# Gated cross-attention and ternary FFN on one core: attention turns of eight heads over two PSUM banks, and a norm over four batches with Newton steps on GpSimd

## The reference

```python
x = x + tanh(g_xattn) * attention(layernorm(x), ctx)   # q from x; k, v from ctx; softmax over the context; @ Wo
x = x + tanh(g_ffn) * (gelu(layernorm(x) @ ternary(W1).T + b1) @ ternary(W2).T + b2)
# layernorm(x) = (x - mean) / sqrt(var + 1e-5), over the 256 columns, no weights
```

## Time and profile before

| | us |
|---|---|
| median of 3 runs (lowest, highest) | 1670.24 (1670.09, 1671.91) |
| the profiled execution, its own time | 1668.12 |
| span of its instructions | 1666.3 |
| PE busy in the span | 1511.3 (91%) |
| DVE busy | 1487.7 (89%) |
| ACT busy | 938.2 (56%) |
| POOL busy | 668.6 (40%) |

### The profile page before, as it was taken

The page is one execution under the profiler, slowest core; times in us unless marked ns, Lnnn a source line. Parts: engine busy times, 40 slices in busy tenths (PEclk is TensorE's granted clock), DMA queues, the critical chain, the costliest instruction groups (busy, mean ns, idle before and its releaser), DMA issues.

```text
span 1666.3 us, 48258 instructions
## 1 busy us (share of the span) xinstructions
PE 1511.3 (91%) x14501; PEld 1010.6 (61%) x14501; DVE 1487.7 (89%) x4375; ACT 938.2 (56%) x1799; POOL 668.6 (40%) x813
## 2 busy tenths in 40 slices
PE   3899999999999999999999999997999999999998
PEld 2566666666666666666666666664666666666665
DVE  7799999999999999999999999987888888888886
ACT  2465656565656666566656565644555554555554
POOL 5355555455554545554555555452111111111111
PEclk9799999999999999999999999986999999999999
DMA  2333333333333333333333333311010110101101
GB/s 79 89 97 85 94 85 86 97 86 97 83 96 83 97 84 93 87 89 92 86 97 83 98 81 97 80 47 55 27 38 25 38 36 27 38 25 38 38 25 51
DMA packets 207471, 117.93 MB, mean 71 GB/s; under 512 B 24912, under 2 KB 207184, under 8 KB 207440
## 3 DMA queue, kind: packets, MB, share of 16 engines
q1 hardware_dynamic: 207440, 117.54, 26.1%
HBM read 32.53 MB, written 16.78 MB: 30 GB/s over the span
## 4 chain that ended last, share of the span: by engine, by line
PE 54%; DVE 26%; issue 13%; ACT 4%; DVEq 2%; DMA 0%; ACTq 0%
PE bank L1060 12%; PE bank L308 9%; PE bank L1090 5%; PE bank L1089 5%; DVE smax L745 5%; PE bank L332 4%; PE bank L315 4%; PE bank L299 4%; DVE xres L790 3%; DVE rstd L685 3%; DVE k L715 2%; DVE rstd L687 2%; PE bank L387 2%; DVE y L1047 2%; DVE rstd L678 2%
## 5 line engine op out<-in xcount | busy, mean ns | idle before, releaser
L915 POOL TENSOR_TENSOR probl<-prob 128x512 f16<-128x512 f32 x512 | 528.9, 1041 | 535.8 <-ACT prob L597 534.9
L597 ACT ACTIVATE prob<-bank,masks 128x512 f32<-128x512 f32 x512 | 345.2, 687 | 144.9 <-PE bank L367 144.9
L745 DVE TENSOR_REDUCE smax<-bank 128x4 f32<-128x512 f32 x512 | 348.1, 681 | 14.5 <-PE bank L332 10.6
L1076 DVE TENSOR_TENSOR hidl<-hid 128x512 f16<-128x512 f32 x256 | 226.9, 886 | 79.5 <-ACT hid L1071 78.8
L1071 ACT ACTIVATE hid<-bank,b_sb 128x512 f32<-128x512 f32 x256 | 175.9, 687 | 212.3 <-PE bank L1060 206.1
L1060 PE MATMUL bank<-y,w1T 128*128 128x512 f16 x1024 | 262.9, 379 | 29.9 <-DVE y L1047 28.4
L1154 POOL TENSOR_TENSOR xres<-xres,b2g 128x1024 f32 (+1 forms) x32 | 75.7, 2365 | 431.3 <-ACT yln L1024 413.4
L1089 PE MATMUL bank<-w2T,hid 128*128 128x256 f16 x1024 | 237.4, 273 | 1.4 <-ACT w2T L1004 1.4
L1090 PE MATMUL bank<-w2T,hidl 128*128 128x256 f16 x1024 | 237.3, 273 | 0.0
L332 PE MATMUL bank<-k_rows,q_rows 34*128 34x128 f16 x2048 | 228.0, 222 | 6.8 <-DMA q_rows<-smaxT 3.4
L367 PE MATMUL bank<-q_rows,k_rows 50*128 50x128 f16 x2048 | 204.4, 221 | 0.9 <-DMA q_rows<-smaxT 0.9
(11 more groups left out here) (90 smaller groups left out, 2555.7 us busy)
## 6 DMA issues: line engine op xcount, KB each, us to landing
q_rows<-q SPq DMA_DIRECT2D x512, 64.0 KB, 2.6
k_rows<-k SPq DMA_DIRECT2D x512, 64.0 KB, 2.5
xres<-in_x_dram SPq DMA_DIRECT2D x64, 256.0 KB, 2.7
out_dram<-ystage SPq DMA_DIRECT2D x32, 512.0 KB, 2.9
ctx_sb<-in_ctx_dram SPq DMA_DIRECT2D x64, 192.0 KB, 3.1
q_rows<-smaxT SPq DMA_DIRECT2D x128, 8.0 KB
w_raw<-in_L_ffn_W_dram SPq DMA_DIRECT2D x2, 1024.0 KB, 6.7
prob<-in_L_xattn_Wq_dram SPq DMA_DIRECT2D x1, 256.0 KB, 3.9
```

Source lines behind the costliest of these rows:

```text
L597: act.activation(prob[u][:], st_bank[u % 2][:], ACT.Exp, bias=0.0, scale=masks[g.parity][:, 2 + b:3 + b]).then_inc(exp_done, 1)
L745: dve.tensor_reduce(smax[:, b, u * UH:(u + 1) * UH], sm_bank[u % 2][:].rearrange("p (h j) -> p h j", h=UH), AX.X, ALU.max).then_inc(max_ta ...
L915: pool.tensor_tensor(probl[u][:], prob[u][:], prob[u][:].bitcast(BF16)[:, 1::2], ALU.subtract).then_inc(prob_split, 1)
```

## The change

- A batch has two turns of eight heads instead of four of four (`PH = 8`, `PAIRS = 2`). A turn's scores fill both banks of a pair (`sm_banks`, `st_banks`), and one `take_max` and one exponential read 1024 columns. Each pair is a single buffer: rough scores wait for the last maximum, scores for the last exponential. `low_prob` still runs on four heads at a time, and `weigh` waits for each half.
- `pe_group` and `dve_group` are written anew in this order. On VectorE, `add_attention` moves from its place behind one `take_max` to behind `take_max`, `round_max`, `low_max`, `read_weighed` and `normalise`, at both of its places in a group.
- The norm of x runs over four batches, once per two groups, in the group of parity 0. VectorE makes statistics and seed (`seed_x`, four parts: `norm(0)` to `norm(3)`), GpSimd the Newton steps (`root_x`, 14 parts, two behind each `low_prob` from the second on). `x` is loaded four batches at a time, and that load waits for `ln_ready`.
- In the FFN the same 14 parts remain on VectorE. The negative half of the variance is made one part earlier, and the wait for `y_done` moves from part 3 to part 12.

```diff
 def pe_group(pe, g, left):
-    scores(pe, g, 0, 0, (g, 1, 2))
+    scores(pe, g, 0, 0, (g, 1, 1))
     if not first:
-        weigh(pe, before, 1, 2)
+        weigh(pe, before, 1, 1)
         tr = project_out(pe, g.batch(0) - 2, tr)
-    scores(pe, g, 0, 1, (g, 1, 3))
-    if not first:
-        weigh(pe, before, 1, 3)
     if left >= 2:
         pe.wait_ge(v_split, g.n + 1)
         project_q(pe, g2, 0)
         tr = transpose_ctx(pe, g2, tr)
         project_q(pe, g2, 1)
-    scores(pe, g, 0, 2, (g1, 0, 0) if left >= 1 else None)
+    scores(pe, g, 0, 1, (g1, 0, 0) if left >= 1 else None)
+    tr = transpose_max(pe, g, 1, tr)
     weigh(pe, g, 0, 0)
-    tr = transpose_max(pe, g, 1, tr)
-    scores(pe, g, 0, 3, (g1, 0, 1) if left >= 1 else None)
-    weigh(pe, g, 0, 1)
...
-    scores(pe, g, 1, 0, (g1, 0, 2) if left >= 1 else None)
-    weigh(pe, g, 0, 2)
+    scores(pe, g, 1, 0, (g1, 0, 1) if left >= 1 else None)
+    weigh(pe, g, 0, 1)
     if not first:
         tr = project_out(pe, g.batch(0) - 1, tr)
-    scores(pe, g, 1, 1, (g1, 0, 3) if left >= 1 else None)
-    weigh(pe, g, 0, 3)
     if left >= 3:
         tr = transpose_x(pe, g.after(3), tr)
...
 def dve_group(dve, g, left):
-    take_max(dve, g, 1, 2)
-    norm(8)
-    if not first:
-        add_attention(dve, g.batch(0) - 2)
-    norm(9)
-    take_max(dve, g, 1, 3)
+    take_max(dve, g, 1, 1)
+    norm(0)
     round_max(dve, g, 1)
-    norm(10)
+    norm(1)
     low_max(dve, g, 1)
+    norm(2)
     if not first:
         read_weighed(dve, g.batch(0) - 1, 1, 1)
+        norm(3)
         normalise(dve, g.batch(0) - 1, 1, 1)
+        add_attention(dve, g.batch(0) - 2)
...
     if left >= 2:
         low_k(dve, g2)
-    if not first:
-        add_attention(dve, g.batch(0) - 1)
     if left >= 1:
-        take_max(dve, g1, 0, 3)
+        take_max(dve, g1, 0, 1)
         round_max(dve, g1, 0)
         low_max(dve, g1, 0)
     read_weighed(dve, g.batch(0), 0, 1)
     normalise(dve, g.batch(0), 0, 1)
+    if not first:
+        add_attention(dve, g.batch(0) - 1)
...
+def seed_x(dve, half, i):
+    past = half - 2
+    if i == 0:
+        dve.wait_ge(x_in, 16 * (half + 1))
+        for b in range(QB):
+            last = dve.bn_stats(stats[:, b, :], row_of(half * QB + b))
+    elif i == 1:
...
+        dve.tensor_copy(rstd[:, 2, :], stats[:, :, 1])
+        for b in range(QB):
+            last = dve.bn_aggr(meanvar[:, b, :], stats[:, b, :])
+    elif i == 2:
...
+        dve.tensor_scalar(newton[:, 2, :], meanvar[:, :, 1], EPS, -0.5, ALU.add, ALU.mult)
+        last = dve.tensor_scalar(newton[:, 0, :], meanvar[:, :, 1], EPS, None, ALU.add)
+    else:
...
+        dve.tensor_scalar(newton[:, 1, :].bitcast(I32), newton[:, 0, :].bitcast(I32), -0.5, RSQRT_SEED,
+                          ALU.mult, ALU.add).then_inc(root_seeded, 1)
+def root_x(pool, half, i):
...
+        elif i % 4 == 1:
+            last = pool.tensor_tensor(t, y, y, ALU.mult)
+        elif i % 4 == 2:
+            last = pool.tensor_tensor(t, t, hv, ALU.mult)
...
 def pool_group(pool, g, left):
     for b in range(2):
         for u in range(UNITS):
             low_prob(pool, g, b, u)
+            k = b * UNITS + u
+            if g.parity == 0 and left >= 4 and k >= 1:
+                for i in range(2 * k - 2, 2 * k):
+                    root_x(pool, g.half + 2, i)
 def sp_group(sp, g, left):
-    if left >= 4:
-        sp.wait_ge(ln_done, x_past)
-        load_x(sp, g.after(4))
+    if g.parity == 1 and left >= 6:
+        sp.wait_ge(ln_ready, x_past)
+        load_x(sp, g.half + 3)
```

More of the change, by code:

```diff
@@ L658, in ln_part @@
         def ln_part(dve, i, rows, step, base, ready):
-            n = len(rows)
-            half, y, t, shift = (rstd[:, k, 0:n] for k in range(4))
+            half, y, t = (rstd[:, k, :] for k in range(3))
             if i > 0:
@@ L693, in row_of, with norm_x @@
             return xres[:, bass.ds(batch, 1), :].rearrange("p o d -> p (o d)")
-        def norm_x(dve, g, parts):
+        def norm_x(dve, half, parts):
             for i in parts:
                 if i == 0:
-                    dve.wait_ge(x_in[g.parity], 16 * (g.half + 1))
-                if i == 3 and not (isinstance(g.half, int) and g.n == 0):
-                    dve.wait_ge(ln_done, 2 * g.n)
-                rows = [row_of(g.batch(b)) for b in range(2)] if i == 0 else (None,) * 2
-                ln_part(dve, i, rows, ln_step, g.n * (LN_PARTS - 1), ln_ready)
+                    dve.wait_ge(x_in, 16 * (half + 1))
+                if i == LN_PARTS - 2 and not (isinstance(half, int) and half == 0):
+                    dve.wait_ge(ln_done, QB * half)
+                rows = [row_of(half * QB + b) for b in range(QB)] if i == 0 else ()
+                ln_part(dve, i, rows, ln_step, half * (LN_PARTS - 1), ln_ready)
@@ L816, in dve_first @@
             dve.wait_ge(mask_set, 1)
-            norm_x(dve, g1, range(LN_PARTS))
             low_q(dve, g0)
@@ L860, in dve_group @@
             if not first:
                 read_weighed(dve, g.batch(0) - 1, 1, 1)
+                norm(3)
                 normalise(dve, g.batch(0) - 1, 1, 1)
-            norm(11)
+                add_attention(dve, g.batch(0) - 2)
+            else:
+                norm(3)
+            norm(4)
             if left >= 2:
                 low_q(dve, g2)
+            norm(5)
+            if left >= 1:
+                take_max(dve, g1, 0, 0)
+            norm(6)
+            read_weighed(dve, g.batch(0), 0, 0)
@@ new lines, in dve_group @@
+            norm(7)
+            normalise(dve, g.batch(0), 0, 0)
+            if left >= 2:
+                low_k(dve, g2)
+            norm(8)
+            if left >= 1:
+                take_max(dve, g1, 0, 1)
+                round_max(dve, g1, 0)
+            norm(9)
+            if left >= 1:
+                low_max(dve, g1, 0)
+            norm(10)
+            read_weighed(dve, g.batch(0), 0, 1)
+            norm(11)
+            normalise(dve, g.batch(0), 0, 1)
+            if not first:
+                add_attention(dve, g.batch(0) - 1)
@@ L1011, in norm_y @@
             for i in parts:
-                if i == 3 and not (isinstance(g.half, int) and g.n == 0):
-                    dve.wait_ge(y_done, QB * g.n)
-                rows = [row_of(g.n * QB + b) for b in range(QB)] if i == 0 else (None,) * QB
+                if i == LN_PARTS - 2:
+                    if isinstance(g.half, int) and g.n == 0:
+                        dve.wait_ge(ln_done, B)
+                    else:
+                        dve.wait_ge(y_done, QB * g.n)
+                rows = [row_of(g.n * QB + b) for b in range(QB)] if i == 0 else ()
                 ln_part(dve, i, rows, y_step, g.n * (LN_PARTS - 1), y_ready)
```

291 lines of the change are left out of this document (147 added, 144 removed).

## The result

The changed kernel takes 2047.35 us (median, 2044.29 to 2051.60) where the kernel before, run beside it, took 1670.16: a ratio of 1.2261 [1.2233, 1.2290], 377 us slower. The forecast was 2120 us, 73 too many. The profiled execution has a span of 2043.8 us at a mean granted clock of 0.822. The whole loss lies in the attention: from the first to the last start of ScalarE's gelu (tile `hid`) the FFN takes 503 us (1533.5 to 2036.1), and before it took 504 (1154.6 to 1658.6).

The account below looks back on a forecast made before the run. The prediction took chains from TensorE through ScalarE and VectorE, closing at the two transposes behind `add_attention`, as the bound. 1668 us plus 234 for later chains plus 222 for low clock gave 2124, say 2120 us; range 1850 to 2300.

Parts of the forecast that it names:

- The place of the loss: TensorE waiting for the late `add_attention` at the context and x transposes, 3 to 6 us a group together.
- First chain: Context transpose begins 4.75 us after ScalarE's `high_v` starts (A), 0.69 later than before; in parity 0 the seed adds 2.5.
- Second chain: x transpose begins 4.39 us after ScalarE's `high_k` starts (B), 2.29 us later than before, in every group.
- The sum at full clock: Attention groups grow 3.9 us on average over 60 groups: 234 us more, 1902 us without any fall of the clock.
- the 0.3 us that were to come back at the changes of turn: TensorE saves 0.3 us a group, between 0 and 0.7, through fewer changes of turn.
- The clock: TensorE's clock falls around the x transpose in most groups, costing 3.7 us a group, 222 us in all.
- five such pieces, two of them hidden: From x transpose to first quarter's end, five slow projection pieces cost 4.7 us; the first wait hides two, leaving 2.8.
- The rival with falls in parity 0 alone: The clock falls only in attention groups of parity 0, giving 2013 us; chance 0.08.
- What was costed at nothing: Exponentials and `low_prob`, `root_x` steps, SP's load of x behind `ln_ready`, single buffers; FFN and start within 5 us.
- The signs named: Profile: transposes wait 3 to 6 us a group, VectorE about 1240 us, below 70% in attention, mean clock near 0.8.
- The rival of three seed operations held up by `low_prob`: Up to three VectorE seed operations each wait for GpSimd's `low_prob`, 3.1 us in 30 groups: 94 us more, 2214 us.

Follow-up runs that it names:

- b1: The kernel before with only both `add_attention` moved behind `normalise`; four-head turns, double buffers and old norm stay: 2220.24 us, ratio 1.3309.
- e4: The changed kernel with useless float32 projections in TensorE's two pauses, the waits for `add_attention` kept: 1901.32 us, ratio 1.1402.
- e5: The changed kernel with both `add_attention` early and the load of x at the end of SyncE's group: 1803.00 us, ratio 1.0824.
- n1: The kernel before with only the new norm (four batches, Newton steps on GpSimd), load of x last in SyncE's group: 1659.15 us, ratio 0.9927.
- e8: e5 with useless float32 products ahead of each x transpose and at two places behind the seed in even groups: 1717.35 us, ratio 1.0294.
- e1: The changed kernel with both `add_attention` back at the head of their chains, the rest kept: 1864.65 us, ratio 1.1186.
- m1: The kernel before with only the eight-head turns, both `add_attention` early and the old norm: 1695.39 us, ratio 1.0164.
- n2: n1 with two useless float32 products at each of two places behind the seed in even groups: 1634.99 us, ratio 0.9792.

## Why the prediction was right, and where it was off

**The place of the loss** was right. b1 shows that the late `add_attention` alone makes a loss of this kind, and the transposes wait 3.8 us a group (3 to 6 were named).

**First chain.** Forecast A + 4.75 in parity 1; it was A + 5.23. The difference is one instruction: `low_max` took 0.92 instead of 0.17 us, and without these 0.75 it would be A + 4.48. In parity 0 it was A + 6.30 against 4.75 + 2.5 = 7.25: the seed cost 6.30 - 4.48 = 1.82, just under its lower bound of 1.9. Its copy took 0.17, where the row of before gave 0.57. That the two errors nearly cancel is luck: over both parities the place moved by (1.17 + 2.24) / 2 = 1.70 us, where 0.69 + 1.25 = 1.94 was forecast.

**Second chain.** Forecast B + 4.39, measured B + 4.30. The maximum of 1024 columns was put at 1.30 and takes 1.217.

**The sum at full clock.** Forecast +234 us; e4 measures +231. This closeness is in part luck. The groups of e4 take 20.2 and 21.3 us in turn, on average 3.9 more than the 16.84 before, as much as the 1.70 and 2.2 by which the two places moved. So the 0.3 us that were to come back at the changes of turn do not show; the two places, some 0.3 us together less late than forecast, make up for them.

**The clock.** This is the term that was mis-sized: 60 x 3.7 = 222 us forecast, 146 measured (2.4 a group). The step "five such pieces, two of them hidden" counted the second `project_q` as slow. In the rows above it runs at 1.03 us, since the clock was back by 727.9, and so it does in 14 of 15 groups between 500 and 860 us. That is 60 x 0.94 = 56 of the 76 us by which the term was too large. The rest is not parted: some stretches were back after only 3.4 us, others lasted 13.7 and more. The mechanism (fall around the x transpose, return in the float32 work of the next group's first half) is in the windows. In 200 to 400 us a mean of 0.78 means 44% of the time at 0.50.

The rival with falls in parity 0 alone does not stand. Groups of parity 1 fall as well: their x transposes at 738.28 and 786.22, behind pauses of 2.49 us, run in 1.11 us instead of 0.65. The Trainium skill (TensorE: Matmul & The Clock Gate, "HAM oscillation — how this bites in real kernels") ties the oscillation to long waits between bursts. The trace agrees as far as the clock oscillates, but here pauses of 0.3 to 0.8 us in a cluster (e5, n1) preceded falls too.

**What was costed at nothing.** In the changed kernel itself it cost nothing that shows. SyncE waits there for `ln_ready` too (55.5 us in 17 times from 200 to 1000 us), but no wait of TensorE for moved rows stands in that stretch, so the late chains cover it. Once they are mended, SyncE's queue behind `ln_ready` is worth 62 us (e5), and of the 133 us left in e5 86 or more are the low clock (e8). That an early `add_attention` would not bring the old time back was not seen: e1 gives back 183 of 377 us.

**The signs named.** Waits, VectorE's share (57%, below 70% was named) and mean clock (0.822, near 0.8) came out. VectorE's busy time fell to 1307.8 us, not 1240: 2.9 us fewer a group (16.0 to 13.1) where some 4 were forecast. The small parts that left had overlapped their neighbours in the busy time: from 400 to 800 us the groups of VectorE's instructions add up to 18.7 us a group before and 14.5 after, 4.2 fewer. The parities differ by 1.07 us at the first place, not 2 to 3, since the seed was shorter and `low_max` longer.

The rival of three seed operations held up by `low_prob` did not come about, and this trace is no test of it: in the pair shown no `low_prob` ran beside the seed's copy at 703.74 (the last two began at 701.42 and took 2.04 us), and all eight copies between 500 and 860 us took 0.17.

**What stays open.** Why m1's pauses nearly always leave the clock at 1.00 (two falls from 200 to 1000 us) and e5's, as large in the window shown, do not. In e5 the seed's pauses come in the group beside them, and filling both places (e8) holds the clock, but no run separates how the two add up.

## What to carry to other kernels

When a change frees an engine that looks full, look first at what stands ahead of the one instruction for which the bounding engine waits: here 2.9 us fewer a group on VectorE lost to some 2 us more ahead of each `add_attention`. Price the late instruction and the clock apart, by filling the pauses with useless matmuls: the run with fillers gives the first, its difference to the run without gives the second. Where a cluster of short pauses precedes a fall, a filler of half a microsecond can be worth more than the work it delays (n2: by the ratios 1.35%, some 22 us, under n1), and the gain of a part (n1's norm) can show only then.

## What the runs showed of the hardware that was not expected

- A VectorE instruction on a 16-column tile, usually 0.17 us, took 0.92 us beside GpSimd's `low_prob`, in every group of parity 1 between 500 and 860 us. In the pair shown it began at 726.21 and ended at 727.13, and GpSimd's two `low_prob`, from 725.07 for 2.04 us, ended at 727.11. The Trainium skill (SBUF — State Buffer, "SBUF: two separate sides") has VectorE and GpSimd share ports that one holds for its whole instruction; for this instruction the trace agrees. Not every small one is held up: `round_max` began beside the same `low_prob` at 726.01 and took 0.17.

```profile
725.07 2.04 POOL L951 TENSOR_TENSOR probl<-prob 128x512 f16<-128x512 f32 x2 [3.15 <-ACT prob L590]
```

- Useless float32 matmuls in the pauses held the clock at 1.00 and made the kernel 146 us faster (e4).
- One maximum over two banks takes 1217 ns against 2 x 681, and one exponential over both 1110 against 2 x 687 (the page of the kernel before).
